# A fused attention, GRU and convolution kernel: the prologue's loads by chunk on two queues, and the sums of squares ahead of the modulation

## The reference

```
# layer 0: attention with a modulated RMS norm, 16 heads of 32
scale, shift = split(emb @ W_emb + b_emb)
xn = rms_norm(x, g_norm) * (1 + scale) + shift          # mean of squares over the 512 features
q, k, v = split(xn @ W_qkv);  q, k = rms_norm by head
o = softmax(q k^T / sqrt(32)) v
x = x + (o + o @ W_out)
# layer 1: GRU over the 512 positions, initial state = the conditioning vector
gi = x_t @ W_ih + b_ih;  gh = h @ W_hh + b_hh
r, z = sigmoid(i_r + h_r), sigmoid(i_z + h_z);  n = tanh(i_n + r * h_n)
h = (1 - z) * n + z * h;   x = x + h
# layers 2 and 3: causal depthwise convolutions of 4 taps
x = x + conv(x, taps = the 4 conditioning vectors);   x = x + (conv(x, the same taps) + b)
```

## Time and profile before

| What | Value |
|---|---|
| median of 3 runs | 2173.09 us (2171.21 to 2173.67) |
| profiled execution, its time | 2174.32 us |
| its span | 2172.5 us |
| TensorE matmul busy | 2095.0 us, 96% |
| VectorE, ScalarE, GpSimd busy | 64%, 54%, 52% |
| mean granted TensorE clock | 0.993 |

### The profile page before, as it was taken

One profiled execution on the slowest core, in us unless ns is written; L12 is line 12 of the kernel. 1 busy time (PEld: TensorE's weight loads), 2 busy tenths in 40 slices (PEclk: granted clock), 3 DMA queues, 4 the chain that ended last, 5 costly groups with the idle time before them and its releaser, 6 DMA issues.

```text
span 2172.5 us, 183175 instructions
## 1 busy us (share of the span) xinstructions
PE 2095.0 (96%) x76232; PEld 1577.3 (73%) x76232; DVE 1386.9 (64%) x5128; ACT 1175.8 (54%) x5996; POOL 1125.8 (52%) x3891
## 2 busy tenths in 40 slices
PE   7999999999989999999999999999999999999997
PEld 2222222222379999999999999999999999998886
DVE  3343444444257777777777777777777777777776
ACT  3444445443245555555555555555555555555554
POOL 0143333333136666666666666666666666666665
PEclk9999999999999999999999999999999999999999
DMA  6000000001121212121222121222122212210001
GB/s 252 2 1 1 1 2 1 1 21 59 33 62 49 57 50 55 49 56 49 70 52 57 49 57 47 57 59 66 48 56 50 55 49 60 66 30 7 5 7 19
DMA packets 217526, 95.89 MB, mean 44 GB/s; under 512 B 170064, under 2 KB 213328, under 8 KB 216656
## 3 DMA queue, kind: packets, MB, share of 16 engines
q1 hardware_dynamic: 217280, 92.56, 16.4%
q10 hardware_dynamic: 144, 2.10, 0.2%
HBM read 26.37 MB, written 12.58 MB: 18 GB/s over the span
## 4 chain that ended last, share of the span: by engine, by line
PE 63%; DVE 8%; issue 1%; POOL 0%; ACT 0%; POOLq 0%; DVEq 0%
PE ps L1154 57%; DVE arena L991 5%; PE ps L1182 4%; PE ps L1193 2%; DVE arena L997 1%; DVE arena L1003 1%; DVE arena L1008 1%; PE ps L1200 0%; POOL arena L1232 0%; DVE arena L1052 0%; POOL arena L1236 0%; POOL arena L1238 0%; ACT ps L1087 0%; PE ps L1202 0%; POOL arena L1242 0%
## 5 line engine op out<-in xcount | busy, mean ns | idle before, releaser
L1154 PE MATMUL ps<-whh,arena 128*4 128x128 f32 (+1 forms) x65536 | 1449.0, 246 | 35.3 <-DVE arena L1008 32.9
L1154 PEld LDWEIGHTS ps<-whh,arena 128*4 128x4 f32 x65536 | 1301.0, 87 | 141.6 <-DVE arena L1008 64.5
L991 DVE STREAM_TRANSPOSE arena<-ps 128x128 f32<-128x128 f32 x1024 | 436.5, 426 | 221.7 <-PE ps L1154 221.6
L1112 ACT ACTIVATE arena<-arena 128x8 f32<-128x8 f32 x1024 | 215.9, 211 | 638.5 <-DVE arena L991 637.2
L1232 POOL TENSOR_TENSOR arena<-tap,seq 128x32 f32<-128x32 f32 x1024 | 231.6, 258 | 227.7 <-DVE seq L1021 227.7
L385 DVE TENSOR_REDUCE top<-ps 128x2 f32<-128x1024 f32 x128 | 150.8, 1220 | 253.1 <-PE ps L632 253.1
L1008 DVE TENSOR_TENSOR_SCAN arena<-arena 128x24 f32<-128x24 f32 x1024 | 213.9, 209 | 145.1 <-ACT arena L1123 145.1
L1087 ACT ACTIVATE ps<-arena 128x128 f32<-128x128 f32 x1026 | 269.7, 263 | 1.1 <-PE ps L1202 1.1
L1232 POOL TENSOR_TENSOR arena<-tap,arena 128x32 f32<-128x32 f32 x1024 | 231.8, 257 | 66.8 <-POOL arena L1242 66.8
L997 DVE STREAM_TRANSPOSE arena<-ps 128x64 f32<-128x64 f32 x1024 | 258.1, 252 | 10.9 <-PE ps L1154 0.8
L223 POOL TENSOR_TENSOR arena<-arena 128x2048 f32<-128x2048 f32 x16 | 72.7, 4544 | 352.3 <-ACT arena L296 352.3
(11 more groups left out here) (95 smaller groups left out, 1391.4 us busy)
## 6 DMA issues: line engine op xcount, KB each, us to landing
arena<-arena SPq DMA_DIRECT2D x216, 114.0 KB, 2.2
arena<-arena SPq DMA_DIRECT2D x112, 128.0 KB, 2.1
arena<-seq SPq DMA_DIRECT2D x224, 55.0 KB, 2.0
arena<-gi_d SPq DMA_DIRECT2D x256, 32.0 KB
gi_d<-arena SPq DMA_DIRECT2D x96, 57.0 KB
seq<-in_x SPq DMA_DIRECT2D x4, 1024.0 KB, 17.6
out<-seq SPq DMA_DIRECT2D x14, 256.0 KB
whh<-in_w_hh SPq DMA_DIRECT2D x1, 3072.0 KB, 21.0
```

The lines of the kernel that those rows point to most:

```text
L991: e.transpose(trn[:, h].rearrange("p q (i c s) -> p q c i s", c=2, s=2)[:, :, :, :, 0], bank[RN[h]][:, 0:P].rearrange("p (q c i) -> p q c ...
L1112: e.activation(r_d0[:, h].rearrange("p (i s) -> p i s", s=2)[:, :, 1], trn[:, h, 0, 0:2 * NH].rearrange("p (i s) -> p i s", s=2)[:, :, 0], ...
L1154: last = e.matmul(bank[dst[h]][32 * G:32 * G + B, 0:n], hv, wv[:, k, gates, G, 64 * h:64 * h + 64], start=False, stop=k2 == 1 and k == C - ...
```

## The change

The load of x of batch 0 is cut into its four chunks: 0 and 1 go first on SyncE's queue, ahead of `vecT`; 2 and 3 go first on ScalarE's. The load of `wemb` is cut into its four chunks k, behind x on ScalarE's queue, and the activation table's load comes behind these six. SyncE waits for the second chunk of `wemb` before it issues `wqk` and everything behind. `squares_x(0)` waits for each chunk on a semaphore of its own. On TensorE `sums_x(0)` comes ahead of the modulation, and the modulation waits for each chunk of `wemb`.

```
-                e.dma_start(seq_cb[:, :, 0, PAD:TP], x[:, :, 0, :]).then_inc(l_x[0], 16)
+                for c in range(0, 2):
+                    e.dma_start(seq_cb[:, c, 0, PAD:TP], x[:, c, 0, :]).then_inc(l_x0[c], 16)
                 e.dma_start(vecT[:].rearrange("p c r -> p (c r)"), vec).then_inc(l_vec, 16)
+                e.wait_ge(l_emb[1], 16)
                 for c in range(2):
                     e.dma_start(wqk[:, c]..., w_qk[:, c, :]).then_inc(l_qk[c], 16)
...
                     for c in range(C):
+                        if b == 0:
+                            e.wait_ge(l_x0[c], 16)
                         e.activation(xsq[:, c], seq_cb[:, c, b, PAD:TP], ACT.Square).then_inc(a_xsq, 1)
...
+                for c in range(2, C):
+                    e.dma_start(seq_cb[:, c, 0, PAD:TP], x[:, c, 0, :]).then_inc(l_x0[c], 16)
+                for k in range(C):
+                    e.dma_start(wemb[:, k]..., w_emb[:, 2 * D * k:2 * D * k + 2 * D]).then_inc(l_emb[k], 16)
                 e.preload_act_table_set("natural_log_exp_and_others")
-                e.dma_start(wemb..., w_emb).then_inc(l_emb, 16)
                 squares_x(0)
...
+                sums_x(0)
                 e.wait_ge(d_const, 4)
                 e.wait_ge(l_vec, 16)
-                e.wait_ge(l_emb, 16)
                 for k in range(C):
+                    e.wait_ge(l_emb[k], 16)
                     for G in range(NG):
                         last = e.matmul(bank[PQ]..., vecT[:, k, 0:B], wemb[:, k, :, G, :], ...)
                 last.then_inc(p_emb, 1)
-                sums_x(0)
                 e.wait_ge(d_turn, 1)
```

More of the change, by code:

```diff
@@ L100, in build @@
         PQ, PK, SS, OB = 4, 5, 6, 7
-        l_vec, l_emb, l_v, l_out = sem("l_vec"), sem("l_emb"), sem("l_v"), sem("l_out")
-        l_x = [sem(f"l_x{b}") for b in range(B)]
+        l_vec, l_v, l_out = sem("l_vec"), sem("l_v"), sem("l_out")
+        l_emb, l_x0 = [[sem(f"{n}{k}") for k in range(C)] for n in ("l_emb", "l_x0_")]
+        l_x = [sem(f"l_x{b}") for b in range(1, B)]
         l_qk = [sem(f"l_qk{c}") for c in range(C)]
@@ L172, in _ @@
                     e.dma_start(wqk[:, c].rearrange("p s k n -> p (s k n)"), w_qk[:, c, :]).then_inc(l_qk[c], 16)
-                e.dma_start(seq_cb[:, :, 1, PAD:TP], x[:, :, 1, :]).then_inc(l_x[1], 16)
+                e.dma_start(seq_cb[:, :, 1, PAD:TP], x[:, :, 1, :]).then_inc(l_x[0], 16)
                 e.dma_start(wout.rearrange("p k n -> p (k n)"), w_out).then_inc(l_out, 16)
                 for b in range(2, B):
-                    e.dma_start(seq_cb[:, :, b, PAD:TP], x[:, :, b, :]).then_inc(l_x[b], 16)
+                    e.dma_start(seq_cb[:, :, b, PAD:TP], x[:, :, b, :]).then_inc(l_x[b - 1], 16)
                 e.dma_start(whh[:].rearrange("p k n -> p (k n)"), w_hh).then_inc(s_whh, 16)
@@ L243, in squares_x @@
                 def squares_x(b):
-                    e.wait_ge(l_x[b], 16)
                     if b:
+                        e.wait_ge(l_x[b - 1], 16)
                         e.wait_ge(p_xs, C * b)
                     for c in range(C):
+                        if b == 0:
+                            e.wait_ge(l_x0[c], 16)
                         e.activation(xsq[:, c], seq_cb[:, c, b, PAD:TP], ACT.Square).then_inc(a_xsq, 1)
@@ L305, in invert @@
                     e.activation(rsum, rsum, ACT.Exp, scale=-1.0).then_inc(a_rsum, 1)
+                for c in range(2, C):
+                    e.dma_start(seq_cb[:, c, 0, PAD:TP], x[:, c, 0, :]).then_inc(l_x0[c], 16)
+                for k in range(C):
+                    e.dma_start(wemb[:, k].rearrange("p q G n -> p (q G n)"), w_emb[:, 2 * D * k:2 * D * k + 2 * D]
+                                ).then_inc(l_emb[k], 16)
                 e.preload_act_table_set("natural_log_exp_and_others")
-                e.dma_start(wemb.rearrange("p k q G n -> p (k q G n)"), w_emb).then_inc(l_emb, 16)
                 squares_x(0)
```

## The result

| What | Before | The changed kernel |
|---|---|---|
| median of 16 runs each, us | 2172.47 | 2170.28 |
| lowest to highest, us | 2169.66 to 2175.4 | 2166.18 to 2171.48 |
| mean of the 16, us | 2172.64 | 2169.30 |
| ratio to before, 95% interval | | 0.9984 [0.9977, 0.9991] |
| profiled execution, its time and span, us | 2174.32, 2172.5 | 2166.8, 2165.0 |

The ratio is worth 3.5 us (2.0 to 5.0), against the 3.8 of the prediction: faster, by less than 0.2%. The median falls by 2.2 and the mean by 3.3, because the runs of both kernels lie in two heaps with nothing between: before's eight at 2169.66 to 2171.85 and eight at 2173.09 to 2175.40, the changed kernel's seven at 2166.18 to 2168.18 (granted clock 0.994 to 0.996) and nine at 2170.07 to 2171.48 (0.993), so that the mean of the lower heap falls by 3.9 us and that of the upper one by 3.3.

A forecast was written before the change was run, and what follows sets the result against it. Late x bounds the first projection; first square 5.05, modulation's end 13.50, `scale_x` 14.57 and projection 16.22 instead of 19.98 save 3.8 us. From the median, 2173.09 - 3.8 = 2169.3 us, range 2166.7 to 2172.6.

The forecast's parts named there:

- The forecast and its case: Whole kernel: 2169.3 us, a saving of 3.8; likeliest case a saving of 1.5 to 4.9 us, chance 0.62.
- What bounds the kernel, and that the saving reaches the end: Start of the first projection: x is late, the modulation early; what the projection gains should reach the end.
- Loads: Start of the program: all of x in at 5.3, last chunk of `wemb` at 10.8, `wqk` of chunk 0 near 12.5.
- the sign that I had named for a lower rate: Squares on ScalarE: the prediction is wrong on rates if they wait for x beyond 5.5.
- The cover that I put at 2.1 us: Modulation on TensorE: fourth chunk of `wemb` wanted at about 12.9, landed at 10.8, so TensorE is the bound.
- The rival of a low rate: Loads: chunks move at a low rate, making it slower; at 165 GB/s the time is 2177.2; chance 0.05.
- ScalarE: Before the squares: six issues at 0.5 each and the table load of 1.28 put the first square at 5.05.
- TensorE: Sums, then modulation: start at 5.82, plus 5.16 of passes, 2.37 of slow start and 0.15 to drain, end at 13.50.
- a slow start of 4.74 us: TensorE's first work: 4.74 us at the lower clock, costing half, 2.37; bounds for the stretch 3.41 and 10.30.
- What follows: After the modulation's end: 1.02 of vector steps, 0.05 to `scale_x` at 14.57, 1.65 to the projection at 16.22.
- SyncE's wait: Wait for the second chunk of `wemb`, ending at about 7.9: costs nothing, no bandwidth lost; without cover at most 6.5 us.
- The clock behind the gap: Gap before the projection, 2.7 us against 3.26: the clock falls as before, 1.7 us of work lost in both.

The follow-up runs named there:

- the run with only the place changed: The changed kernel plus 19 tiny matmuls of zeros (32 columns) ahead of the sums, while TensorE waits for x: 2174.29 us, ratio 1.0011 to before.
- The run with all three: The changed kernel with the table load first, 9 matmuls of zeros ahead of the sums and 10 in the gap before the projection: 2170.08 us, ratio 0.9994 to before.
- the two runs with all three: The run with all three (2170.08 us), and the same with 13 tiny matmuls more, 32 additional in all (2166.85 us).

## Why the prediction was right

**The forecast and its case.** I gave a saving of 3.8 and a chance of 0.62 to no difference that can be told; measured 3.5 by the ratio (0.16%, with an interval that leaves out no change, but under the 0.2% that the prediction called tellable), 4.57 at the projection of the profiled execution, and 4.17 (15.81) in the run with only the place changed, whose prologue does the same work. The range was said to be widened by about 1 us on each side; its bounds of 2166.7 and 2172.6 are 0.9 and 0.5 beyond the savings of 5.5 and 1.0. The medians and means measured, 2170.28 and 2169.30, lie well inside.

**What bounds the kernel, and that the saving reaches the end.** Right. After the projection's start no load appears among TensorE's waits in the changed kernel either; from the mark on the rounds run alike but for the one round at the lower clock.

**Loads.** The order came out as said, the rate somewhat lower. x was complete at about 6.2 (expected 5.3), so the second square waited 0.16, until 6.04, which is the sign that I had named for a lower rate; it cost nothing, since TensorE wants that square at about 7.7; the last `wemb` landed at 11.5 (10.8), `wqk` of chunk 0 at about 13.9 (12.5). The cover that I put at 2.1 us was only 0.6: the fourth chunk is taken up at about 12.1. The run with all three shows the price when it is gone, a wait of 0.54. The rival of a low rate did not come: with chunks of 256 and 512 KB the loads ran at 404, 385, 410 and 410 GB/s from 6 to 10 us. The Trainium skill's rule of 1 MiB or more in a DMA ("DMA: Bandwidth & Descriptors", Measured), which I had set against the change, did not bind here: these rates were reached with three to seven transfers issued and not yet landed.

**ScalarE.** Six issues took 0.74 to 3.93 and the first square came at 5.25, 0.2 after the 5.05 predicted. Both ends of my range (4.45 and 7.57) were wide.

**TensorE.** This is the term that was mis-sized. I took a slow start of 4.74 us from the one row that showed one; in this execution it was 2.7. Half of the 2.0 between them, 1.0 us, is saved; the first square, 0.2 late, took 0.2 of it back, and what is left, 0.8, is the difference between 4.57 and 3.8. Other executions with the sums first, and nothing on TensorE just ahead of them, show 3.8, 4.9, 5.3, 5.6 and 5.7, so 4.74 was a fair middle and the single execution a lucky one. The modulation itself ends as long after as was worked out: 6.02 + 5.16 + 1.35 + 0.15 = 12.68.

**What follows.** 1.05 from there to `scale_x` and 1.65 to the projection, as predicted.

**SyncE's wait.** I costed it at nothing and argued that it takes no bandwidth. That was right, and it was too little said: the run without it shows that it protects `wemb` and carries the change.

**The clock behind the gap.** It fell as before, and I left it in place. The same gap of 2.7 us passed without a fall in two executions (the order alone, and the table load first) and with one in four others (the changed kernel, the one without SyncE's wait, TensorE kept busy before the sums, and only the place); with matmuls in the gap the clock stayed up in four of four. What decides between the two with the gap left open is not shown.

## What to carry to other kernels

When loads bound the start, write down for each consumer what it needs and when, and give the bytes in that order; a queue beside it that wasn't held back took about half of the rate here, whatever its bytes were worth. Whether the cut into chunks is needed, or the order of the bytes alone would do, no run here tells apart. Changing only the loads or only the order of the work brought nothing or cost 2.8 us here, so a reordering is to be judged with its loads. And before a gain or loss of 3 us in 2170 is put down to an edit, compare the stretches that the edit doesn't touch: the clock in one round and the place of a loop's instructions each moved as much as the change did.

## What the runs showed of the hardware that I had not expected

- The place of a loop's instructions has a price. With 19 matmuls more ahead of it, the last loop's step takes 3.08 to 3.09 instead of 3.03 us, at full clock and with the same work, in all three kernels that had 19; with 0, 9 and 32 it doesn't. The time lies in TensorE's own stretch of the step: it is busy 175.60 of 186.00 us there in the kernel with only the place changed, and 170.79 of 182.34 in the changed kernel, 0.07 us more a step. The Trainium skill ("Runtime: NRT & Kernel Launch", Instruction fetch mechanics) says that instructions are fetched in blocks and that a taken branch to outside the blocks at hand forces a fetch. The traces don't bear this out as the cause: the queues that the profile names `instruction` moved three packets in a window of 200 us around the last 64 steps, in the changed kernel (first pair of rows) as in the run with all three (second pair), where a fetch at each step would make some 64. The cause stays open.

```profile
q8 instruction: 2, 0.03, 0.1%
q14 instruction: 1, 0.01, 0.0%
...
q8 instruction: 2, 0.03, 0.1%
q14 instruction: 1, 0.01, 0.0%
```

- The view of stretches printed 1.00 for the changed kernel from 6 to 8 us, while a pass of 512 columns took 0.86 us (7.70 to 8.56); from 9.08 to 9.51 it took 0.43. So up to the first change of the clock in a trace that column says nothing here; the distance between weight loads does.
- TensorE's slow start differs from one execution to the next, 2.7 to 5.6 us with the same kind of work, and even nine matmuls from 2.01 on had not ended it by 5.97 in two of the four executions that had them (sums of 4.38 and 3.93; in the two runs with all three, 3.64, it was over). What it costs in a prologue is known only to within 1.5 us.
